# Routing folded into one pipeline over batches, with row numbers scattered to lists in DRAM instead of a table of marks

## The reference, cut to what matters

```python
# second layer: small[i] added to every column j that the path visits with row i
contrib = small[i_idx] * valid[:, None]
expanded = jnp.zeros((T_large, d)).at[j_idx].add(contrib)
x = x + expanded
...
# third layer: inputs = layernorm(x), 16*256 = 4096 rows, 64 experts, 2 for each row
gate_logits = jnp.einsum('te,ex->tx', x, gate_kernel)
weights, selected = jax.lax.top_k(gate_logits, TOP_K)
weights = jax.nn.softmax(weights.astype(jnp.float32), axis=-1)
flat_experts = selected.reshape(-1)
sort_idx = jnp.argsort(flat_experts)
sorted_x = jnp.take(x, sort_idx // TOP_K, axis=0)
group_sizes = jnp.bincount(flat_experts, length=NUM_EXPERTS).astype(jnp.int32)
h0 = jax.lax.ragged_dot(sorted_x, w0, group_sizes)
h1 = jax.lax.ragged_dot(sorted_x, w1, group_sizes)
out_sorted = jax.lax.ragged_dot(jax.nn.silu(h0) * h1, wo, group_sizes)
```

## Time and profile before

| | us |
|---|---|
| median of 3 runs (lowest 1440.59, highest 1442.3) | 1441.71 |
| the profiled execution, own time | 1440.14 |
| its span, first to last instruction | 1438.4 |
| PE busy in the span | 989.3 (69%) |
| DVE busy | 947.8 (66%) |
| POOL busy | 631.2 (44%) |
| ACT busy | 583.6 (41%) |

### The profile page before, as it was taken

The page is one execution under the profiler, slowest core; times in us unless marked ns, Lnnn a source line. Parts: engine busy times, 40 slices in busy tenths (PEclk is TensorE's granted clock), DMA queues, the critical chain, the costliest instruction groups (busy, mean ns, idle before and its releaser), DMA issues. The chain is left out here.

```text
span 1438.4 us, 20758 instructions
## 1 busy us (share of the span) xinstructions
PE 989.3 (69%) x6537; PEld 896.2 (62%) x6537; DVE 947.8 (66%) x1936; ACT 583.6 (41%) x1319; POOL 631.2 (44%) x558
## 2 busy tenths in 40 slices
PE   3667777777787761776003692479999999999960
PEld 1566766667677651666002481469999998888850
DVE  1999999999999941888886866923333332322227
ACT  3768777787877641443003450512121211111110
POOL 5877787868778711000002301033445544444410
PEclk8899999999999995555556975789999999999985
DMA  6544545556465511113030033127888988788729
GB/s 198 185 146 127 178 139 178 172 143 191 138 185 168 156 29 35 30 30 59 0 117 0 0 117 114 62 82 265 268 276 277 284 286 272 256 269 286 261 68 347
DMA packets 172663, 230.00 MB, mean 160 GB/s; under 512 B 43836, under 2 KB 97612, under 8 KB 171984
## 3 DMA queue, kind: packets, MB, share of 16 engines
q1 hardware_dynamic: 152636, 205.95, 46.6%
q0 software_dynamic: 13072, 18.22, 4.2%
q10 hardware_dynamic: 6852, 4.57, 1.0%
HBM read 202.32 MB, written 22.11 MB: 156 GB/s over the span
## 5 line engine op out<-in xcount | busy, mean ns | idle before, releaser
L846 PE MATMUL st_y_ps<-ident,st_hc 128*128 128x128 f32 x2048 | 273.9, 291 | 116.3 <-DVE st_hc L489 116.2
L846 PEld LDWEIGHTS st_y_ps<-ident,st_hc 128*128 128x128 f32 x2048 | 255.9, 203 | 139.6 <-DVE st_hc L489 138.8
L371 POOL TENSOR_TENSOR st_u<-st_dx,codes 128x1024 f32<-128x1024 f32 x128 | 298.9, 2361 | 37.7 <-DVE st_h L481 37.2
L481 DVE TENSOR_TENSOR_SCAN st_h<-st_da,st_u 128x512 f32<-128x512 f32 x256 | 297.6, 1203 | 9.7 <-POOL st_u L371 9.6
L1954 PE MATMUL mo_h<-mo_xt,w 128*128 128x128 f32 (+31 forms) x2048 | 279.1, 287 | 1.7 <-DVE mo_xt L2051 1.7
L1954 PEld LDWEIGHTS mo_h<-mo_xt,w 128*128 128x128 f32 x2048 | 269.6, 192 | 6.8 <-issue 2.4
L2057 DVE TENSOR_TENSOR mo_inter<-mo_silu,mo_h 128x128 f32<-128x128 f32 (+31 forms) x256 | 75.3, 298 | 272.6 <-ACT mo_silu L2028 224.4
L2028 ACT ACTIVATE mo_silu<-mo_h 128x128 f32<-128x128 f32 (+31 forms) x256 | 72.1, 286 | 312.3 <-PE mo_h L1954 208.8
L612 ACT ACTIVATE st_da<-st_delta,st_a_neg 128x510 f32<-128x510 f32 x256 | 171.7, 685 | 66.4 <-DVE st_h L481 59.6
L1894 POOL DMA_INDIRECT outs<-mo_o,choice x95 | 99.5, 1048 | 214.7 <-DVE mo_o L2068 198.2
L489 DVE TENSOR_TENSOR st_hc<-st_h,st_cps 128x1024 f32<-128x1024 f32 x128 | 152.5, 1192 | 0.0
(11 more groups left out here) (311 smaller groups left out, 1325.2 us busy)
## 6 DMA issues: line engine op xcount, KB each, us to landing
codes<-bc SPq DMA_DIRECT2D x256, 256.0 KB, 4.0
w<-in_L_ffn_w_dram SPq DMA_DIRECT2D x128, 512.0 KB
wo<-in_L_ffn_wo_dram SPq DMA_DIRECT2D x64, 512.0 KB
co_got<-outs SPq DMA_DIRECT2D x16, 512.0 KB, 6.2
x<-in_x_dram SPq DMA_DIRECT2D x8, 512.0 KB, 9.0
st_cx<-in_ctx_dram SPq DMA_DIRECT2D x8, 512.0 KB, 4.9
dist<-st_dd SPq DMA_DIRECT2D x8, 512.0 KB, 4.9
codes<-wv_code SPq DMA_DIRECT2D x32, 128.0 KB, 3.4
```

Of the source, the lines that this page charges most:

```text
L371: nc.gpsimd.tensor_tensor(u_sb[k % URING][:, :, :], dx[p % 2][:, :, :], over_chunks(b_sb[k % BRING]), ALU.mult).then_inc(u_ok, 1)
L481: nc.vector.tensor_tensor_scan(h_sb[k % HRING][:, dh, :], da_ps[dh][:, :], u_sb[k % URING][:, dh, :], 0.0, ALU.mult, ALU.add).then_inc(h_o ...
L846: m = nc.tensor.matmul(y_ps[t // 2][:, t % 2, dh * P:(dh + 1) * P], hc_sb[k % RING][:, dh, t * P:(t + 1) * P], K.ident[:, :], start=False, ...
```

## The change

`expand` and `route` become one block. Its loops are written out, and one loop over beats replaces the two passes and most of route: in beat b, DVE adds batch b to `K.x` and takes its statistics and scale factors, makes the mask of batch b+1, finds the two largest logits of batch b-2 and marks them one-hot, and works out for batch b-3 the rank of each entry within its expert. The mask is now one comparison of a squared distance: ACT squares (2 instructions per batch instead of 4), DVE compares; POOL's product is gone. The statistics are aggregated batch by batch, the square root is ACT's and five small operations per batch on POOL refine it (`newton`). ACT, no longer DVE, takes the turned rows out of PSUM; DVE reads the logits from PSUM itself, so ACT's copy of them is gone.

The place of an entry is now its expert times `CAP` plus its rank. Per batch POOL issues four indirect DMAs (`enter`), each of which scatters 128 numbers of 4 bytes to such places in `bucket`, a list per expert in DRAM; SP fills the lists beforehand with numbers of vacant rows. When all 64 scatters have landed and the order is known, POOL fetches the first 256 numbers of each expert's list in order of rank (one indirect DMA of 64 rows of 1 KB), DVE casts them, PE turns them twice, and DVE copies them into `K.choice` and `K.table`. The table of marks, the places and the large one-hot tables are gone.

In `experts`, ranks 32 to 63 all get 128 places. The tile of the last rank is now always served first in the loop at the end, and the entry numbers of its later trips are read from `bucket` by SP. The stages before `expand` are unchanged; `combine` too.

```diff
-ROOMS = ((0, 2, 1, 220, 20), (2, 14, 2, 190, 6), (16, 16, 2, 148, 2), (32, 4, 4, 128, 0), (36, 28, 2, 126, 2))
+ROOMS = ((0, 2, 1, 220, 20), (2, 14, 2, 190, 6), (16, 16, 2, 148, 2), (32, 32, 32, 128, 0))
...
         @block.sync
         def _(sp):
+            sp.wait_ge(constant, VACANT)
+            sp.dma_start(K.bucket_dram.rearrange("(p j) a -> p (j a)", p=P), vacant[:, :]).then_inc(vacated, 16)
+            for b in range(B):
+                sp.wait_ge(xn_ok, b + 1)
...
+            sp.wait_ge(row_ok, ORDER)
+            for k in range(WRING):
+                load_weights(K, sp, expert_at(K, sp, k), k)
...
         @block.gpsimd
         def _(pool):
...
+            nc.gpsimd.iota(vacant[:, 0:LINES // L * L], [[0, LINES // L], [1, L]], base=2 * TOK,
+                           channel_multiplier=L).then_inc(constant, 1)
...
+            def newton(b):
+                u = b % 2
+                pool.wait_ge(rough_ok, b + 1)
+                nc.gpsimd.tensor_tensor(root[u][:, :], rough[u][:, :], rough[u][:, :], ALU.mult).then_inc(fine, 1)
...
+            def enter(b):
+                pool.wait_ge(slot_ok, b + 1)
+                if b == 0:
+                    pool.wait_ge(vacated, 16)
+                for t in range(2 * b, 2 * b + 2):
+                    for i in range(2):
+                        nc.gpsimd.indirect_dma_start(
+                            K.bucket_dram[:, :], bass.IndirectOffsetOnAxis(ap=slot[:, t, i:i + 1], axis=0),
+                            row[:, t, i:i + 1], None).then_inc(placed, 16)
...
+            newton(0)
+            routing_constants()
+            for b in range(1, B + 4):
+                if real(b):
+                    newton(b)
+                if real(b - 3):
+                    enter(b - 3)
+            pool.wait_ge(row_ok, ORDER)
+            pool.wait_ge(placed, ENTERED)
+            nc.gpsimd.indirect_dma_start(entries_i[:, :], None,
+                                         K.bucket_dram.rearrange("(l j) a -> l (j a)", j=2 * P),
+                                         bass.IndirectOffsetOnAxis(ap=lines[:, :], axis=0)).then_inc(placed, 16)
...
         @block.scalar
         def _(act):
+            for b in beats:
+                if real(b - 2):
+                    take_turned(b - 2)
+                if real(b - 1):
+                    normalize(b - 1)
+                if real(b + 2):
+                    far(b + 2)
+                if real(b):
+                    roots(b)
...
         @block.tensor
         def _(pe):
+            pe.wait_ge(constant, FLOW)
+            for b in range(B + 4):
+                if real(b):
+                    expanded(b)
+                if real(b - 2):
+                    logits(b - 2)
+                if real(b - 3):
+                    rank(b - 3)
+                if real(b - 1):
+                    turn(b - 1)
...
-            for k in range(groups):
-                pe.wait_ge(marks, 2 * k + 2)
-                pe.wait_ge(entered_ok, (k + 1) * MG)
-                for i in range(MG):
-                    m = nc.tensor.matmul(table_ps[:, 0:MT], at_lo[k % 2][:, i, :], entered[k % 2][:, i, :],
-                                         start=(k == 0 and i == 0), stop=(k == groups - 1 and i == MG - 1))
-                m.then_inc(used, 1)
```

889 lines of the change are left out of this document (421 added, 468 removed).

## The result

The changed kernel takes **1431.09 us** (median of 8 runs, 1425.91 to 1437.43); the kernel before, timed beside it, 1445.51 us (8 runs, 1440.59 to 1449.58). The ratio is 0.9903, with a 95% interval of 0.9876 to 0.993: 14.4 us less. The forecast was 1416.5 in a range of 1400 to 1432, which was 25.2 us under the 1441.71 then known. So the time lies at the upper edge of the range and a little over half of the gain came. The profiled execution took 1432.94 us, its span is 1431.2.

A forecast was written before the change was run, and what follows sets the result against it. No engine is full through the 175.2 us routing stretch; in the new pipeline POOL's scatters set the pace. -30.9 + 3 + 1.5 + 1 + 0.2 = -25.2 from 1440.14 gives 1414.9, as median 1416.5; range 1400 to 1432.

The forecast's parts named there:

- The stretch: From POOL's first iota of expand to PE's first turn of gathered rows: 144.3 us against 175.2, 30.9 us less.
- Constants and fill: Start of the stretch: 3.7 us of constants, then 21.6 until batch 0's first scatter.
- POOL's end: End of the scatter pipeline, at +124.9: twelve batches at 6.6 us and four at 5.1 after constants and fill.
- Last scatter to fetch: Tail: the last scatter lands 5.7 us after its issue, 4.7 after POOL's end.
- border: Tail, between the table and the first gather: 1.35 us, as in the kernel before.
- first gather: End of the tail, up to PE's first turn of gathered rows: 5.65 us, as in the kernel before.
- The order of experts: Known at about +115, so the first expert's weights, 6.4 us, hide behind the tail.
- The two allowances of that stretch: Added to the stretch: 3 us for DVE and POOL blocking each other, 1.5 for PE not holding full clock.
- Rival 2: Scatters dear beside DVE: 1431 at 1.5 us each, 1463 at 2.0; chance 0.12 (1.4 to 1.6) and 0.09 (1.7 and over).
- rival 3: Scatters cheap: a 4-byte piece costs POOL 0.9 us, the refinement loop sets a 5.2 us pace, 1394; chance 0.10.
- Rival 1: PE at half clock in the pipeline: pace 7.1 us a batch, 8 us more, 1424; chance 0.16.
- Experts: Experts stage: 128 places for ranks 36 to 62 cost PE 1 us at most; added gather and scatter rows lie beside PE.

The follow-up runs named there:

- quiet set: Sets of runs in which the unedited kernel before took 1417 to 1420 us; its trace shows no idle before the wide down product.
- loud sets: Sets of runs in which the unedited kernel before took 1436 to 1446 us, the changed kernel's first runs among them.
- r16: Changed kernel without the experts' gathers after the first four, whose rows are used again, save the last rank's; 1393.24 us, 0.9688 of the kernel before.
- r13: Changed kernel moving only 126 falling to 100 rows for ranks 36 to 62, engines still working on 128; 1409.62 us, 0.9797 of the kernel before.
- r10: Changed kernel, unedited, run again where the kernel before took 1416.79 us; 1397.03 us, 0.9862 of the kernel before.
- r14: Changed kernel with engines working on only 126 falling to 100 rows for ranks 36 to 62, 128 rows still moved; 1418.57 us, 0.9867.
- r15: Changed kernel without the experts' weight loads after the first four, whose sets are used again; 1416.72 us, 0.9851 of the kernel before.
- r9: Kernel before, unedited, run again against itself; 1420.43 us, ratio 1.003.
- r11: Changed kernel with the kernel before's rooms for ranks 36 to 62 (126 falling to 100 rows); 1391.25 us, 0.9817 of the kernel before.

## Why the prediction was right and where it failed

- **The stretch: right in its mechanism and nearly in its sum.** Constants and fill 27.1 us (25.3 forecast), POOL's end at +124.3 (+124.9), a batch 6.4 us apart by POOL's refinements over twelve batches (6.6). Last scatter to fetch 2.5 (4.7), fetch to cast 4.8 (5.7), cast to table 1.4 (2.0), border 2.2 (1.35), first gather 8.1 with the weights streaming beside it at 285 GB/s (5.65). Sum 143.3, forecast 144.3 without allowances and 148.8 with them. That the sum is so near is partly luck: fill and pipeline err by 1.8 and -2.3 us, and the errors in the tail (from -2.2 to +2.4) cancel. The order of experts came at +116.8 (+115), and POOL, which waited for no one from 803 to 901 (75.7 us busy, the rest the gaps between issues), set the pace as said.
- **The two allowances of that stretch, 3 and 1.5 us, had nothing to pay for.** Indirect issues kept their 1.27 us from start to start (1.34 behind the first of a batch). With DVE busy 58.9 of 97.3 us hardly a scatter was held: median 962 ns, least 957, one at 1217. Rival 2 is dead by that row, and rival 3 too: a 4-byte piece costs POOL what a 1 KB piece does. The Trainium skill (SBUF — State Buffer, "SBUF: two separate sides") has VectorE and GpSimd share a port pair that VectorE locks for whole instructions of its two-port modes. The trace shows no such hold on these 64 issues, but it is hardly a test of the rule: the masks that I counted as locking took 0.35 us for 256 columns, where they had taken 0.41 for 512, so they ran far below the old rate, and no row shows that they were in such a mode.
- **Rival 1 half happened and cost nothing.** PE went back and forth between half and full clock through the pipeline (0.75 in the mean; turns of 3.4 to 10.2 us at either level from 811.8 to 876.7, half from there on), and the additions on DVE still came at POOL's pace: two of them are 6.57 us apart.
- **The step that failed is the term "Experts", sized 1 us, which was 21.7.** I priced the 128 places by PE's columns alone and let the added rows "lie beside PE". (They are 392 each way, not 366.) The columns did cost little: 1.3 us in the narrow experts' sum in the quiet set, 3.1 in the loud one. But what the change did to POOL's DMAs reached PE: in the loud sets the wide experts went from 240.8 to 255.7 us, in the quiet one by 1.1. The end of the stage took 3.7 in both, where I had 0.2; that makes 3.1 + 14.9 + 3.7 = 21.7. It was not that more rows weighed more, as I had thought of them: moving 128 rows took POOL *less* time than 122 or 118, so its gathers fell earlier, into the wide experts' up product. In the trace of before, the sign was there to read: 14.2 us of idle stood before L1968, in experts whose ranks and work I took as fixed. I read the stage as PE busy 425 of 443 and did not ask what the remaining 17 waited for, and whether the change reaches it.
- That the time lies inside the range is luck. Its upper part was there for dear scatters and half clock, which took no time here; the experts' stage took the gain, and the stretch was 5.5 us better than with its allowances.
- In the quiet set the same sum reads -30.8 + 6.1, with 4.7 from a later start and 0.2 in the combine: -19.9 in span. Without the late marks the forecast's mechanism holds and its Experts term is short by 5 us; with them it is short by 20 in this pair of traces.

## What to carry to other kernels

Padding is not priced by the engine that computes on it alone: it also changes what each gather and scatter costs the engine that issues it, here downwards, and so when the later ones go out. An engine off the critical path can hurt by being earlier. Where a stage that "does not change" has idle time, find its releaser before calling the stage fixed. And compare a kernel with the one before in the same set of runs only: the unedited kernel's median moves by 16 to 29 us between the two kinds here, no less than the whole change gains.

## What the runs showed of the hardware

- **PE's semaphore marks can come late by up to about 3.5 us, in some sets of runs only.** In the wide experts of the loud sets the second silu starts up to 4.6 us after the first (often 1.5, 2.9 or 4.4), where the products are 0.9 to 1.2 us apart; PE's own matmul rows show nothing, only ACT's idle before the silu and the semaphore's updates do. With the gathers out none was late but the one beside the last gather left (r16), and in the quiet sets none was. (In the very first expert the silus stand 1.5 to 2.9 us apart in every trace, so it tells nothing.) What differs between the sets is not shown.
- Late marks go with two gathers issued 0.8 to 1.3 us and 2.1 to 2.5 us after the first silu; where POOL was later and the first of them stood at 1.8 us or more, the second silu came after 1.1 to 1.5 us (r13, 6 wide experts) or 1.1 to 1.7 (before, 6). With the first at 1.5 to 1.7 us it was both (1.0 to 2.4 in r13). The first experts are an exception: some had early gathers and no late mark. That is seen in the traces and wasn't tested in a loud set.
- The issue of an indirect DMA on POOL does not get cheaper with fewer rows: 0.95 to 1.03 us for 128 rows, 1.71 for 122, 1.34 for 124, 1.31 for 116, 0.98 for 112 (traces of before and after). The Trainium skill (DMA: Bandwidth & Descriptors, "Why a DMA increments its semaphore by 16 and not by 1") says that the number of DMA engines used is the largest one up to 16 that divides the slowest dimension of both sides; with the rows as that dimension it would be 16 for 128 and 112 rows, 14 for 126, 4 for 124 and 116, 2 for 122. The trace agrees so far as the issues are dear just where that number is small; on which DMA engines the rows went it doesn't show.
- GpSimd's drain at the end of the stage takes 7.82 us with 128 rows moved for every narrow expert and 5.62 with fewer (r10, r14, r15 against r9, r11, r13).
- A 4-byte scatter from POOL costs the same 0.96 us + 0.30 as a gather of 1 KB rows, and the fetch that waited for the last one began 3.4 us after its issue.
